# Rows of the second layer norm in a recurrent layer, moved from VectorE to ScalarE with a GpSimd shift

## The reference

```python
def _layernorm(x, axis=-1, eps=1e-05):
    m = jnp.mean(x, axis=axis, keepdims=True)
    v = jnp.var(x, axis=axis, keepdims=True)
    return (x - m) / jnp.sqrt(v + eps)
# L1_attn: xt = layernorm(x); K, V, R = projections of mixes of xt and its shifted rows
#          S = scan(S * decay + K); y = (R * (S * first + K) * V) @ Wo;  returns x + y
x = _layernorm(x + _L1_attn_ref(x, ...))          # its rows are called x4 in the kernel
x = _layernorm(x + _L1_xattn_ref(x, ctx, ctx, ...))  # its rows are called x5
x = _layernorm(x + _L1_ffn_ref(x, ...))
```

## Time and profile before

| | |
|---|---|
| median of 3 runs | 1298.01 us |
| the profiled execution, its time | 1300.81 us |
| the profiled execution, its span | 1298.40 us |
| recurrent stage in the profile | about 929 to 1047 us |
| busy in the whole span: PE, VectorE, ScalarE, GpSimd | 88%, 54%, 45%, 36% |

### The profile page before, as it was taken

How to read it: one execution, slowest core, us unless ns; L and a number is a source line. 1 busy time by engine, 2 the same in 40 slices (tenths; PEclk the granted TensorE clock), 3 DMA queues, 4 the chain that set the end, 5 groups by cost and what they waited for, 6 DMA issues and landing times. The chain is left out here.

```text
span 1298.4 us, 23672 instructions
## 1 busy us (share of the span) xinstructions
PE 1139.4 (88%) x7485; PEld 826.5 (64%) x7526; DVE 697.5 (54%) x1886; ACT 585.0 (45%) x1071; POOL 470.5 (36%) x906
## 2 busy tenths in 40 slices
PE   7799898999877876999999999999889677998991
PEld 4344444444344443889999999988556446997951
DVE  4766666767354643622323232339787755453647
ACT  3267677677755643222323232334243222555720
POOL 7445332231422322013333332302341575705456
PEclk9599999999988997999999999999999668998996
DMA  9900100000000006501111011132330125756633
GB/s 354 355 3 17 83 1 1 1 1 1 2 1 1 1 1 228 232 17 34 41 34 42 34 42 34 38 129 74 119 101 1 38 77 182 246 181 195 204 110 118
DMA packets 68127, 109.31 MB, mean 84 GB/s; under 512 B 7345, under 2 KB 54962, under 8 KB 65202
## 3 DMA queue, kind: packets, MB, share of 16 engines
q1 hardware_dynamic: 58130, 80.96, 18.2%
q0 software_dynamic: 9888, 27.01, 6.5%
HBM read 65.61 MB, written 42.34 MB: 83 GB/s over the span
## 5 line engine op out<-in xcount | busy, mean ns | idle before, releaser
L1451 ACT ACTIVATE f_work<-op_R,f_ub 128x128 f32<-128x128 f32 x312 | 89.2, 369 | 204.1 <-PE op_R L1791 204.1
L513 ACT ACTIVATE att_PT<-att_RB 128x1024 f32<-128x1024 f32 (+1 forms) x192 | 148.1, 808 | 66.0 <-PE att_RB L652 34.6
L558 DVE CUSTOM_DVE_ANT_0 att_junk<-att_RB,att_causal_q 128x128 f32<-128x128 f32 (+3 forms) x256 | 120.6, 488 | 52.9 <-PE att_RB L634 43.7
L1791 PEld LDWEIGHTS op_R<-f_work,f_xTf 128*128 128x128 f32 x1248 | 145.3, 192 | 3.9 <-DVE f_work L1581 2.0
L1791 PE MATMUL op_R<-f_work,f_xTf 128*128 128x128 f32 x1248 | 145.8, 275 | 1.5 <-DVE f_work L1581 1.5
L1800 PE MATMUL op_R<-wd_down,f_work 128*128 x624 | 141.1, 379 | 0.0
L634 PE MATMUL att_RB<-att_kT,att_qT 96*128 96x512 bf16 (+3 forms) x384 | 120.7, 351 | 20.3 <-DVE att_mx L558 6.6
L1800 PEld LDWEIGHTS op_R<-wd_down,f_work 128*128 128x128 f32 x624 | 115.5, 190 | 14.1
L1590 DVE COPY f_xTf<-wu_up 128x1024 f32 x78 | 54.1, 695 | 106.5 <-PE op_R L1791 98.8
L1394 POOL DMA_INDIRECT Yd<-f_work,f_inv x39 | 38.5, 987 | 196.3 <-DVE f_work L1600 196.3
L634 PEld LDWEIGHTS att_RB<-att_kT,att_qT 96*128 96x128 bf16 x384 | 34.4, 100 | 110.0 <-issue 38.8
(11 more groups left out here) (480 smaller groups left out, 2151.0 us busy)
## 6 DMA issues: line engine op xcount, KB each, us to landing
Xd<-g_zero SPq DMA_DIRECT2D x1, 12032.0 KB, 41.1
f_xin<-Xd SPq DMA_DIRECT2D x47, 256.0 KB
Yd<-f_yo SPq DMA_DIRECT2D x47, 256.0 KB
wu_up<-up_w SPq DMA_DIRECT2D x9, 1024.0 KB, 9.6
wd_down<-down_w SPq DMA_DIRECT2D x9, 1024.0 KB, 18.5
w_all<-w SPq DMA_DIRECT2D x6, 768.0 KB, 8.3
wd_down<-Yd SPq DMA_DIRECT2D x16, 256.0 KB, 5.3
w_all<-w SPq DMA_DIRECT2D x1, 2304.0 KB, 17.7
```

The lines of the kernel that those rows point to most:

```text
L513: act.activation(buf[:, :, 0:w], ST[:, 2 * (k % 2):2 * (k % 2) + 2, 0:w], ACT.Exp, scale=float(HD) ** -0.5).then_inc(exp_done, 1)
L558: dve.tensor_tensor_reduce(junk[:, k % RING, 0:w], RB[:, bank, 0:w], G.causal_q[:, 512 - w:512], 1.0, LOWEST, ALU.add, ALU.max, to).then_i ...
L1451: last = act.activation(hT[:, u % 2, m, :], bank[:, UB + m // 4, (m % 4) * P:(m % 4 + 1) * P], ACT.Gelu, bias=ub[:, ds(e, 1), m])
L1791: mm = pe.matmul(bank[:, UB + n, P * m:P * (m + 1)], staged_up[:, kk, at:at + P], xT[:, u % 2, kk, :], start=(kk == 0), stop=(kk == KD - 1))
```

## The change

GpSimd makes the shift for this norm as it did for the other two. The rows of x4 are written by ScalarE as an activation with scale rstd and bias shift, no longer by VectorE; the step keeps its place in the list, so on ScalarE it stands behind `xn` and ahead of `x5` and `tx`. VectorE waits in `y` for the x4 of the quarter before, since it writes over `xr[1]`.

```diff
                 pool.wait_ge(var_ready[n], k)
                 ch.link(pool.tensor_scalar(rstd[n][p][:, j], mv[n][p][:, j, 1], LN_EPS, None, ALU.add))
-                if n == 1:
-                    pool.tensor_tensor(rstd[n][p][:, j], rstd[n][p][:, j], half[:, j], ALU.pow).then_inc(rstd_ready[n], 1)
-                else:
-                    ch.done(pool.tensor_scalar(shift[n][p][:, j], mv[n][p][:, j, 0], -1.0, None, ALU.mult))
-                    ch.link(pool.tensor_tensor(rstd[n][p][:, j], rstd[n][p][:, j], half[:, j], ALU.pow))
-                    pool.tensor_tensor(shift[n][p][:, j], shift[n][p][:, j], rstd[n][p][:, j], ALU.mult).then_inc(rstd_ready[n], 1)
+                ch.done(pool.tensor_scalar(shift[n][p][:, j], mv[n][p][:, j, 0], -1.0, None, ALU.mult))
+                ch.link(pool.tensor_tensor(rstd[n][p][:, j], rstd[n][p][:, j], half[:, j], ALU.pow))
+                pool.tensor_tensor(shift[n][p][:, j], shift[n][p][:, j], rstd[n][p][:, j], ALU.mult).then_inc(rstd_ready[n], 1)
...
+                if what == "x4":
+                    act.wait_ge(rstd_ready[1], 2 * q + k + 1)
+                    for j in (2 * k, 2 * k + 1):
+                        last = act.activation(G.x_sb[:, q * J + j, :], xr[1][:, j, :], ACT.Identity,
+                                              bias=shift[1][p][:, j:j + 1], scale=rstd[1][p][:, j:j + 1])
+                    last.then_inc(x4_ready, 1)
                 if what == "x5":
                     act.wait_ge(rstd_ready[2], 2 * q + k + 1)
...
                 if what == "y":
                     filled(dve, step)
+                    if q:
+                        dve.wait_ge(x4_ready, 2 * (q - 1) + k + 1)
                     j = slice(2 * k, 2 * k + 2)
...
-                if what == "x4":
-                    dve.wait_ge(rstd_ready[1], 2 * q + k + 1)
-                    for j in (2 * k, 2 * k + 1):
-                        last = dve.tensor_scalar(G.x_sb[:, q * J + j, :], xr[1][:, j, :], mv[1][p][:, j, 0:1],
-                                                 rstd[1][p][:, j:j + 1], ALU.subtract, ALU.mult)
-                    last.then_inc(x4_ready, 1)
```

## The result

The changed kernel takes 1306.0 us, the median of 8 runs (1305.23 to 1311.06); the kernel before, run beside it, 1297.95 us. The ratio is 1.0062, 95% interval 1.0046 to 1.0077, so the change costs 8.05 us. The forecast was 1304.3 us, +6.3, in a range of 1301.0 to 1308.5.

The account below looks back on a forecast made before the run. TensorE's path from y's statistics through x4 to the scores was taken to bound each joint, not VectorE. Joints 0 to 3 add 0.73 + 0.72 + 2.1 + 2.75 = 6.3 us to 1298.01, giving 1304.3 us, range 1301.0 to 1308.5.

Parts of the forecast that it names:

- What bounds the joint: Behind x4, TensorE's path from statistics to scores sets the joint; VectorE's load is cover with 2.03 us to spare.
- The longer path, 0.73 and 0.72: Joints 0 and 1: GpSimd's longer chain and ScalarE's slower pair add 0.73 and 0.72 us.
- The shift's share: Every joint: GpSimd's two more small instructions for the shift add 0.37 us to the path.
- GpSimd unstretched beside the scan: Second x4 half: GpSimd's instructions take no stretch beside VectorE's scan; otherwise the joint would cost 1.3 us more.
- Joint 1's slide of x5 is hidden: Joint 1: x5 delays the tx copies to 974.2 to 975.3, hidden by 1.8 us since projections run until 977.1.
- Joint 2, +2.1: Joint 2: x5 delays the tx copies, tg turns wait for their banks, value projections start late; +2.1 us instead of +0.7.
- Joint 3, +3.1, of which 0.35 comes back: Joint 3: tx copies behind x5 delay the scores 3.1 us; GpSimd gives back 0.35, leaving +2.75.
- Rival 4: TensorE's clock falls in a longer gap; with GpSimd stretching 1306 to 1308.5 us; chance 0.12.
- main case: Forecast as worked out, all four joints' terms, 1304.3 us; own range 1302.8 to 1306; chance 0.62.
- Rival 1: VectorE bounds the joints, so scans 1.88 us earlier come back at joints 0 to 2; 1292.4 us; chance 0.07.
- Rival 2: Only the longer path counts, ScalarE's new x5 order hides somewhere; sum 3.1 us, 1301.1 us; chance 0.10.
- Rival 3: Nothing to be seen, within 2.6 us, if ScalarE's pair or GpSimd's shift also overlaps better; 1299 us; chance 0.09.

Follow-up runs that it names:

- one filler: Changed kernel plus eight idle-time matmuls of 256 columns on TensorE ahead of its x4 wait at joint 1 alone; ratio 1.0039 to the kernel before.
- both repairs: Changed kernel with x5 ahead of x4 in the list and eight idle-time TensorE matmuls before joint 1's x4 wait; ratio 1.0019 to the kernel before.
- the shift alone: Kernel before with GpSimd's shift made but not used, VectorE still writing x4; ratio 1.0053 to the kernel before.
- x5 first: Changed kernel with the two x5 steps ahead of the two x4 steps in the list; ratio 1.0044 to the kernel before.
- shift and filler: Kernel before with GpSimd's unused shift and eight idle-time TensorE matmuls at joint 1; ratio 1.0024 to the kernel before.
- fillers at all joints: Changed kernel plus idle-time TensorE matmuls before the x4 wait, 8 at joints 1 and 2, 16 at joint 3; ratio 1.0044 to the kernel before.
- x4 late on ScalarE: Changed kernel with x5 ahead of x4, and TensorE's turns tn and value projections ahead of tx; ratio 1.0002 to the kernel before.

## Why the prediction was right, and where it was short

The direction, the place and the mechanism are right and the range holds the time; 8.05 us were measured for 6.3.

- *What bounds the joint.* VectorE's load is cover behind x4: right. Its idle time at joint 1 grew from 2.03 to 6.95 us with the clock, and the scans' earlier start gave nothing. The prediction had put some 4.6 us; the other 2.3 are the clock.
- *The longer path, 0.73 and 0.72.* Measured at joint 0: +0.73. At joint 1, with the gap filled: +0.72. The shift's share was put at 0.37 and is 0.44 at joint 0. GpSimd unstretched beside the scan: right (0.22 us).
- *Joint 1's slide of x5 is hidden.* Right: the copies end at 980.1 and the scores start at 984.37.
- *Joint 2, +2.1.* Measured 1.84 to the start of the projections, and +1.85 for the whole joint in the profile where the clock stayed up (one filler); 2.3 and 2.6 in the two of the changed kernel itself, where the gate product was slower (4.10 and 4.43 us for 3.64).
- *Joint 3, +3.1, of which 0.35 comes back.* Measured +2.94 and 0.36 back, 2.58 for 2.75.
- *The term that was mis-sized is joint 1.* It was put at 0.72 and is 3.04 and 2.40 in the two profiles. Rival 4 had the clock, with a chance of 0.12 and 1306 to 1308.5 us. It read the fall from the stretch after a gap of four microseconds, looked for such a gap at joint 2 alone, and took its price from eight projections. The clock fell at joint 1, which of the first three joints has the longest gap (2.25 us) before the change; the forecast's own working had put 0.5 us more on this gap and never asked what the clock does. So the 1306.0 us that were measured hold a part of rival 4: they lie at the upper end of the main case's own 1302.8 to 1306, and the total lies within the range because the 2 to 3 us that were not foreseen are small beside its width. That much of it was luck. Without the clock the terms measured are 0.73 + 0.72 + 1.85 + 2.58 = 5.9, with the forecast's 6.3 beside them (joints 2 and 3 were each put a little high), and the filler kernel's stage is 6.0 longer.
- *Rival 1* (VectorE is the bound) fell with the 6.95 us of idle time. *Rival 2* (only the path) was the time of the kernel with both repairs. *Rival 3* did not occur. *Rival 4* did in part, at another joint and without its stretching of GpSimd.

## What to carry to other kernels

A busy share says which engine is full, and the timeline behind the moved step says whether it is full there; move work off an engine only where that engine is what the next step waits for. A step moved to another in-order engine also moves everything that stands behind it in that engine's queue: here four activations whose data had long been ready stood in front of two copies, and cost 1.1 us at joint 2 and 1.7 at joint 3, in the stage 2.5 us beside the 3.5 of the longer path at all joints. And where a change makes a gap on TensorE longer, however little, allow for a fall of the granted clock behind this gap: here half a microsecond of wait cost about two more.

## What had not been expected of the hardware

At joint 1 the clock stayed at full in both profiles of the kernel before, with a gap of 2.25 us ahead of the turns and 0.72 between them. It fell in all four profiles with a longer gap and no filler: the changed kernel twice (2.77 and 2.76 us), the shift alone (2.38, and 1.17 between the turns), and x5 first, whose joint 1 also took 11.22 us. The price there was 1.7 to 2.3 us. Fillers in that gap kept the clock up at joint 1 in four profiles of four. The gap ahead is not the whole of it. At joint 2 the clock fell with the shift alone, behind gaps of 0.83 and 1.17 us, and stayed up behind the same gaps in the kernel with shift and filler. And in three profiles (fillers at all joints, both repairs, x4 late on ScalarE) it fell in an output product with nothing ahead of it but 0.91 us in front of the weighted sum, which the other profiles have too: 5.41 us instead of 3.72. What exactly makes it fall stays open.
